# A graph network in two relational layers: which edge rows of layer one are picked by a product instead of gathered, and when they are used

## The chip, the cores and the metric

The kernel runs on one core of a Trainium2 chip. The metric is the device time of one execution in microseconds, the median over several runs.

## The reference, cut to what matters

`h` starts as `relu(layernorm(x))` (3125 nodes, 128 features). Two relational layers follow, over 100,000 edges sorted by destination `dst`, and behind them a GCN part of two convolutions, which the change doesn't touch. A relational layer is

```python
c = comp[etype]                                   # 200 relations, 8 bases
for b in range(num_bases):                        # 8
    xb = h @ V[b]
    m = m + c[:, b, None] * xb[src]
m = m * norm
agg = jax.ops.segment_sum(m, dst, num_segments=h.shape[0])
out = agg + bias + h @ loop_w
```

## The kernel before, in words

The kernel sums over edges first and multiplies by `V` afterwards. Edges come in 784 tiles of 128, in the order of their destination; 8 tiles are a chunk `c` (98 of them), 4 chunks (`j` = 0 to 3) belong to a group `g` of 128 destination nodes (25 groups). A tile needs the rows `h[src]` of its 128 edges. They land in a ring of 8 chunks. **GpSimd** fetches them with one indirect DMA for each tile (`chunk`, L831; the first chunks at L286 and L854); ahead of each chunk it waits until TensorE has finished the chunk five before it (`edges_done`).

Some tiles are not gathered but *picked*. VectorE compares the 128 source numbers of the tile with all 3200 node numbers (`make_pick`, L1016, in two halves of 13 and 12 blocks of 128 nodes, h = 0 and h = 1), which gives 25 one-hot blocks; TensorE multiplies each by the rows of `h`, split in three bf16 parts (25 products of 384 columns, all into the one bank `ps_p`); VectorE adds the three parts into the ring's slot (`keep_picked`, L1032). In layer one (`layer == 0` in the code) the last tile of every odd chunk from 5 to 95 is picked: 46 tiles, two picks a group. The pick for an odd chunk is multiplied in that chunk and the one before it, in sixths (`pick_sixth`, L1280): three pieces in each chunk. There is one buffer `pick` and one bank, so a half is only written when the previous pick's same half was multiplied, and the first product of a pick waits until the previous one was kept (`row_ready`).

In each chunk of layer one VectorE, in order, makes the one-hot edge types (L474), the match with the nodes (L972), `lo` (L978, which waits until TensorE has begun the chunk before: `m_free`), the weights `C` (L993), `M` (L983, called the keys below), then a row to keep and a half of a pick, then the sums of the coefficients (L489, L494); in the third chunk it folds the degrees of the group before (L1061 to L1063), and in the fourth it waits for their product on TensorE (L1252) and keeps it (L1067). TensorE, in order: eight products `lo` x `M` (`sum_slab`, L1219), of which the first waits for the keys, a sixth, the type products (L483), a sixth, in the fourth chunk the degrees' product, four of the chunk's eight edge tiles (L1342), a sixth, the other four tiles. In the second chunk the group's output products stand ahead (L563 to L565). ScalarE copies the results out of PSUM. The last edge tile of an odd chunk is the picked one, so its products wait for `keep_picked`, which VectorE does in the *next* chunk, behind that chunk's keys.

The groups run in a hardware loop of two groups (parity 0 and 1), with a few groups written out at either end. Layer two (`layer == 1`) has picks of its own and begins when layer one is done. SyncE issues the loads of the edge types, of the source numbers of a pick (L877), and the stores of finished slabs, in one queue.

## Time and profile before

| | us |
|---|---|
| median of 3 runs (1999.92 to 2003.72) | 2001.1 |
| the profiled execution | 1999.43 |
| its span, from the first to the last instruction | 1997.8 |
| TensorE busy in it | 1727.5 |
| VectorE busy | 1493.0 |
| GpSimd busy | 1383.6 |

Layer one runs from about 85 to 990 us, layer two and the GCN part behind it. Busy times are of a whole kernel whose parts have different limits, so they tell little about one part; the waits of a stretch, and which of them ends last, tell more.

### The profile page before, as it was taken

Reading aid. Unit: us, or ns where it says so; the run is one execution under the profiler, and the core shown is the slowest. Engines: PE = TensorE matmul, PEld = TensorE weight load, DVE = VectorE, ACT = ScalarE, POOL = GpSimd, SP = SyncE. Lnnn points to the kernel's source line nnn. Section 1 sums busy time; section 2 is a strip of 40 time slices with the busy share of each in tenths; the row PEclk is TensorE's granted clock in tenths of the full one; section 3 lists DMA queues with packets and bytes.
Section 4 is the critical chain, followed back from the end, with each engine's and each line's share of the span. In section 5 each row is a group of like instructions: output and inputs, shape, how many; then the busy total and the mean of one; then the engine's idle time right before and its main releaser. Section 6 shows DMA issues by size and latency. Waiting matters only on the chain. (4 is left out here: it accounts for less than half of the span.)

```text
span 1997.8 us, 41905 instructions
## 1 busy us (share of the span) xinstructions
PE 1727.5 (86%) x12855; PEld 1237.7 (62%) x12856; DVE 1493.0 (75%) x2360; ACT 357.1 (18%) x869; POOL 1383.6 (69%) x1505
## 2 busy tenths in 40 slices
PE   1488888888888888888659999999999999999998
PEld 1366656556556556556537777767667676676564
DVE  7898888888888888887478888877777777652533
ACT  2032222222222222222201011101011010011300
POOL 5777777777777777777477777777777777777000
PEclk8589989889889889988779999999999999989999
DMA  5334334334334334333222222233333322325473
GB/s 151 92 98 114 96 99 109 94 98 110 94 97 108 95 97 109 95 96 88 70 60 64 63 64 64 63 85 86 86 101 93 86 80 80 115 57 167 154 240 120
DMA packets 196506, 196.71 MB, mean 98 GB/s; under 512 B 109132, under 2 KB 160089, under 8 KB 196410
## 3 DMA queue, kind: packets, MB, share of 16 engines
q0 software_dynamic: 45056, 92.36, 18.1%
q1 hardware_dynamic: 143302, 99.03, 17.2%
q10 hardware_dynamic: 8052, 4.04, 0.7%
q8 instruction: 59, 0.97, 0.2%
q14 instruction: 37, 0.30, 0.0%
HBM read 169.75 MB, written 25.57 MB: 98 GB/s over the span
## 5 line engine op out<-in xcount | busy, mean ns | idle before, releaser
L831 POOL DMA_INDIRECT ring<-h_rows,rel_idx x1292 | 1239.8, 960 | 387.9 <-issue 360.2
L1016 DVE TENSOR_TENSOR rel_pick<-rel_src_row,dve_bank 128x1664 bf16<-128x1664 int32 (+1 forms) x268 | 486.2, 1815 | 104.0 <-PE rel_ps_p L1267 56.5
L1342 PE MATMUL rel_ps_z<-rel_C,ring 128*128 128x56 f32 x3100 | 404.1, 278 | 95.2 <-DVE ring L1032 76.3
L1342 PEld LDWEIGHTS rel_ps_z<-rel_C,ring 128*128 128x128 f32 x3100 | 392.1, 197 | 136.6 <-issue 125.8
L1267 PE MATMUL rel_ps_p<-rel_h_parts,rel_pick 128*128 128x384 bf16 x1650 | 283.7, 328 | 24.3 <-DVE rel_h_parts L1004 22.0
L1440 ACT ACTIVATE rel_ZT<-rel_ps_z 128x304 f32 x292 | 114.2, 426 | 1028.6 <-PE rel_ps_z L1342 1023.1
L1280 PE MATMUL rel_ps_p<-rel_h_parts,rel_pick 128*128 128x384 bf16 x1150 | 264.8, 361 | 0.0
L1267 PEld LDWEIGHTS rel_ps_p<-rel_h_parts,rel_pick 128*128 128x128 bf16 x1650 | 158.6, 100 | 138.3 <-issue 30.5
L1430 ACT ACTIVATE rel_A<-rel_ps_a 128x500 f32 x292 | 165.5, 603 | 387.3 <-PE rel_ps_a L1219 209.5
L1219 PE MATMUL rel_ps_a<-rel_M,rel_lo 128*128 128x175 bf16 x784 | 156.3, 299 | 37.1 <-DVE rel_M L983 36.9
L1267 PE MATMUL carried<-rel_h_parts,rel_pick 128*128 128x384 bf16 x1100 | 186.2, 326 | 2.4 <-DVE rel_pick L1016 2.4
L983 DVE TENSOR_TENSOR rel_M<-dve_bank,key_table 128x1400 bf16<-128x1400 f32 x98 | 157.3, 1605 | 0.0
L1267 PEld LDWEIGHTS carried<-rel_h_parts,rel_pick 128*128 128x128 bf16 x1100 | 105.9, 98 | 71.0 <-DVE rel_pick L1016 2.8
L1280 PEld LDWEIGHTS rel_ps_p<-rel_h_parts,rel_pick 128*128 128x128 bf16 x1150 | 113.5, 112 | 56.6 <-issue 22.1
L1219 PEld LDWEIGHTS rel_ps_a<-rel_M,rel_lo 128*128 128x128 bf16 x784 | 77.3, 109 | 105.9 <-issue 61.8
L854 POOL DMA_INDIRECT ring<-h_rows,idx_table x100 | 101.8, 1018 | 56.0 <-issue 33.6
L978 DVE TENSOR_TENSOR rel_lo<-dve_bank,src_lo_table 128x1024 bf16<-128x1024 f32 x98 | 119.4, 1218 | 27.2 <-PE rel_ps_a L1211 27.2
L993 DVE TENSOR_TENSOR rel_C<-dve_bank,coef 128x448 f32<-128x448 f32 x196 | 121.4, 619 | 14.4 <-PE rel_ps_z L1347 2.5
L483 PE MATMUL rel_ps<-comp_parts,rel_onehot 100*128 100x48 bf16 x1568 | 63.3, 193 | 46.3 <-DVE rel_onehot L474 28.6
L483 PEld LDWEIGHTS rel_ps<-comp_parts,rel_onehot 100*128 100x128 bf16 x1568 | 61.2, 103 | 66.1 <-DVE rel_onehot L474 28.8
L474 DVE TENSOR_SCALAR rel_onehot<-rel_types,type_id 100x1024 bf16<-100x1024 bf16 x196 | 91.8, 510 | 10.4 <-DMA rel_types<-edge_types 5.9
L1026 DVE TENSOR_TENSOR rel_pick<-rel_extra_row,dve_bank 128x1664 bf16<-128x1664 int32 (+1 forms) x44 | 79.9, 1816 | 19.6 <-PE carried L1267 19.6
(233 smaller groups left out, 1776.1 us busy)
## 6 DMA issues: line engine op xcount, KB each, us to landing
ring<-h_rows,rel_idx POOLq DMA_INDIRECT x1292
A_slabs<-rel_A SPq DMA_DIRECT2D x25, 800.0 KB
A_slot<-A_slabs SPq DMA_DIRECT2D x25, 800.0 KB, 4.5
rel_types<-edge_types SPq DMA_DIRECT2D x97, 200.0 KB
early_slot<-A_slabs SPq DMA_DIRECT2D x18, 896.0 KB, 6.3
rel_src_row<-in_src_dram SPq DMA_DIRECT2D x134, 64.0 KB, 3.0
last_slot<-A_slabs SPq DMA_DIRECT2D x4, 512.0 KB, 5.5
ring<-h_rows,idx_table POOLq DMA_INDIRECT x116
```

What stands on the lines that cost most here:

```text
L483: ins = self.nc.tensor.matmul(self.ps[:, e * 6 * NB:(e + 1) * 6 * NB], self.onehot[:, s, h, e * P:(e + 1) * P], flat(self.t.comp[:, h, :, ...
L831: g_.indirect_dma_start(ring[:, s * CHUNK + i, :], None, rows_in, bass.IndirectOffsetOnAxis(ap=idx[which][:, n:n + 1], axis=0)).then_inc(l ...
L978: v.tensor_tensor(lo[s][:, :, :], lows.unsqueeze(1).to_broadcast(shape), t.src_lo[:, bass.ds(c * CHUNK, CHUNK)].unsqueeze(2).to_broadcast( ...
L983: v.tensor_tensor(M[s][:, :, :], keys.unsqueeze(1).to_broadcast(shape), t.key[:, bass.ds(c * CHUNK, CHUNK)].unsqueeze(2).to_broadcast(shap ...
L993: v.tensor_tensor(C[s][:, :, :, :], match[s].unsqueeze(2).to_broadcast(shape), t.coef[layer][:, bass.ds(first, CHUNK), :].unsqueeze(3).to_ ...
L1016: v.tensor_tensor(pick[:, b0:b0 + n, :], src_row[s][:, :].unsqueeze(1).to_broadcast(shape), node_ids[:, b0:b0 + n].unsqueeze(2).to_broadca ...
L1219: ins = m_.matmul(into[:, :, bass.ds(half_at[h][i], TW)], lo[s][:, h * HALF + i, :], keyed(s, h * HALF + i), start=False, stop=(i == HALF ...
L1267: ins = m_.matmul(ps_p[s][:, 0:3 * P], pick[:, b, :], h_parts[:, b, :, :].rearrange("p c n -> p (c n)"), start=(b == 0), stop=(b == SRC_BL ...
L1280: ins = m_.matmul(ps_p[0][:, 0:3 * P], pick[:, b, :], h_parts[:, b, :, :].rearrange("p c n -> p (c n)"), start=(b == 0), stop=(b == SRC_BL ...
L1342: ins = m_.matmul(bank(ps_z[s], NB)[:, :, bass.ds(at[i], TW)], ring[:, first + i, :], C[s][:, i, :, :], start=False, stop=(i == n - 1))
L1430: ins = s_.activation(A[into][:, :, bass.ds(column, HN)], half_bank(ps_a[h]), ACT.Copy)
L1440: ins = s_.activation(ZT[into][:, :, bass.ds(column, CN)], bank(ps_z[s], NB), ACT.Copy)
```

## The change

Picked rows are used one chunk later: the pick that is multiplied in chunks j and j + 1 now stands for the last tile of chunk j + 2, an even one, and the even chunks gather 7 tiles, the odd ones 8. In every second group (parity 1, the odd ones) one more tile is picked, the last of its fourth chunk: this *third* pick is made from a buffer of its own (`extra_row`), is multiplied whole in the third chunk, in quarters of 7, 6, 6 and 6 blocks (`pick_quarter`), and the group's last ordinary pick is multiplied whole in the fourth chunk. That is 12 tiles more that are picked and 12 gathers fewer (4 x 7 + 3 x 8 + 7 = 59 in 8 chunks, where 60 were). The core of the diff; the waits of SyncE's loads, the semaphore counts of the ring and the calls follow from it:

```diff
@@ order of picks, and which tile of a chunk is not gathered
-        def number(g, j):
-            return 2 * g - 2 + j // 2
+        def number(g, j, parity, pair):
+            return 2 * g - 2 + j // 2 + pair + (1 if parity == 1 and j == 3 else 0)
+        def nearby(g, j, parity, by):
+            parity, pair = (parity + by) % 2, loop[1] + (parity + by) // 2
+            return number(g + by, j, parity, pair)
+        def is_third(parity, j):
+            return layer == 0 and parity == 1 and j == 2
@@ gathers
-            return CHUNK if late else CHUNK - (1 if layer == 1 else s % 2)
+            return CHUNK if late else CHUNK - (1 if layer == 1 or s == THIRD else 1 - s % 2)
@@ SyncE
+                def load_third(g, before):
+                    after(sp, pick_ready, before)
+                    rows = io["src"].rearrange("(a n) -> a n", a=1)
+                    sp.dma_start(extra_row[:, :], rows[:, bass.ds((g * CPG + 3) * (CHUNK * P) + (CHUNK - 1) * P, P)].to_broadcast([P, P]))\
+                      .then_inc(extra_in, 16)
+                            if parity == 0 and j == 0 and not is_group(g, GROUPS - 1):
+                                load_third(g + 1, 2 * nearby(g, 3, parity, -1) + 2)
@@ VectorE, a chunk of layer one
+                        third = nearby(g, 2, parity, 0)
                         if j % 2 == 0:
-                            behind = (g, 1) if j == 2 else (g - 1, 3)
                             if not (isinstance(g, int) and not first_picks(c - 1)):
-                                keep_picked(number(*behind), 0, (parity * CPG + j - 1) % SLOTS_RING * CHUNK + CHUNK - 1)
-                            if not (isinstance(g, int) and not first_picks(c + 1)):
-                                make_pick(number(g, j + 1), j // 2, g - 1, (1,))
+                                behind = nearby(g, 1, parity, 0) if j == 2 else nearby(g, 3, parity, -1)
+                                keep_picked(behind, 0, (parity * CPG + j) * CHUNK + CHUNK - 1)
+                            if is_third(parity, j):
+                                make_extra(third, loop[1], 1)
+                            elif not (isinstance(g, int) and not first_picks(c + 1)):
+                                make_pick(nearby(g, j + 1, parity, 0), j // 2, g - 1, (1,))
+                        elif parity == 1 and j == 1:
+                            make_extra(third, loop[1], 0)
+                        elif parity == 1:
+                            keep_picked(third, 0, THIRD * CHUNK + CHUNK - 1)
+                            make_pick(nearby(g, 3, parity, 0), 1, g - 1, (1,))
+                        elif j == 1:
+                            if not (isinstance(g, int) and not first_picks(c + 2)):
+                                make_pick(nearby(g, 3, parity, 0), 1, g - 1, (0,))
                         else:
-                            ahead = (g, 3) if j == 1 else (g + 1, 1)
-                            if not (isinstance(g, int) and not first_picks(c + 2)):
-                                make_pick(number(*ahead), ahead[1] // 2, ahead[0] - 1, (0,))
+                            make_pick(nearby(g, 1, parity, 1), 0, g, (0,))
...
+                    if is_third(parity, j):
+                        make_pick(nearby(g, 3, parity, 0), 1, g - 1, (0,))
                     if layer == 0 and j == 3 and not is_first:
                         keep_deg(g - 1)
+                        if parity == 1 and not is_group(g, GROUPS - 2):
+                            make_pick(nearby(g, 1, parity, 1), 0, g, (0,))
@@ TensorE
+PICK_QUARTERS = ((0, 7), (7, 13), (13, 19), (19, 25))
+            def pick_quarter(c, which):
+                b0, b1 = PICK_QUARTERS[which]
+                if which == 0:
+                    after(pe, row_ready, c)
+                if which % 2 == 0:
+                    pe.wait_ge(pick_ready, 2 * c + (1 + which // 2))
+                for b in range(b0, b1):
+                    ins = m_.matmul(ps_p[0][:, 0:3 * P], pick[:, b, :], h_parts[:, b, :, :].rearrange("p c n -> p (c n)"),
+                                    start=(b == 0), stop=(b == SRC_BLOCKS - 1))
+                if which % 2:
+                    ins.then_inc(picked, 1)
+                    quarters = picks_here and parity == 1 and j >= 2
...
-                        if layer == 0 and i == CHUNK - 1 and j % 2 == 1 and not (isinstance(c, int) and not first_picks(c)):
-                            pe.wait_ge(row_ready, number(g, j) + 1)
+                        if layer == 0 and i == CHUNK - 1 and j % 2 == 0 and not (isinstance(c, int) and not first_picks(c - 1)):
+                            pe.wait_ge(row_ready, (nearby(g, 1, parity, 0) if j == 2 else nearby(g, 3, parity, -1)) + 1)
+                        if layer == 0 and i == CHUNK - 1 and j == 3 and parity == 1:
+                            pe.wait_ge(row_ready, nearby(g, 2, parity, 0) + 1)
```

**VectorE, end of the fourth chunk of an odd group.** The rows of before: the second coefficient product, the degrees that it waits for, the loop's branch and the next group's types.

```order
L494 TENSOR_TENSOR coef<-rel_summed,norm_table 128x64
L1067 REGISTER_ALU [waits rel0_deg_done]
L1067 TENSOR_SCALAR deg<-rel_ps_h 128x1
L727 REGISTER_ALU
L727 COMPARE_AND_BRANCH
L474 TENSOR_SCALAR rel_onehot<-rel_types,type_id 100x1024 [waits rel0_types_in2,rel0_product_done]
```

The same place now:

```order
L496 TENSOR_TENSOR coef<-rel_summed,norm_table 128x64
L1089 REGISTER_ALU [waits rel0_deg_done]
L1089 TENSOR_SCALAR deg<-rel_ps_h 128x1
L92 ISA [waits rel0_src_row_in0]
L1038 TENSOR_TENSOR rel_pick<-rel_src_row,dve_bank 128x1664 [waits rel0_picked]
L729 REGISTER_ALU
L729 COMPARE_AND_BRANCH
L476 TENSOR_SCALAR rel_onehot<-rel_types,type_id 100x1024 [waits rel0_types_in2,rel0_product_done]
```

The first half of the next group's pick, which stood ahead of the coefficients, is made behind the degrees.

**VectorE, from the fold of the degrees (third chunk of an odd group) to the fourth chunk's types.** Before:

```order
L1061 TENSOR_TENSOR rel_A<-rel_A 128x12x128 [waits rel0_deg_done,rel0_a_out]
L1061 TENSOR_TENSOR rel_A<-rel_A 128x6x128 [waits rel0_deg_chain]
L1061 TENSOR_TENSOR rel_A<-rel_A 128x3x128 [waits rel0_deg_chain]
L1062 TENSOR_TENSOR rel_A<-rel_A 128x2x128 [waits rel0_deg_chain]
L1063 TENSOR_TENSOR rel_deg_sum<-rel_A 128x128 [waits rel0_deg_chain]
L474 TENSOR_SCALAR rel_onehot<-rel_types,type_id 100x1024 [waits rel0_types_in1,rel0_product_done]
```

Now:

```order
L1083 TENSOR_TENSOR rel_A<-rel_A 128x12x128 [waits rel0_deg_done,rel0_a_out]
L1083 TENSOR_TENSOR rel_A<-rel_A 128x6x128 [waits rel0_deg_chain]
L1083 TENSOR_TENSOR rel_A<-rel_A 128x3x128 [waits rel0_deg_chain]
L1084 TENSOR_TENSOR rel_A<-rel_A 128x2x128 [waits rel0_deg_chain]
L1085 TENSOR_TENSOR rel_deg_sum<-rel_A 128x128 [waits rel0_deg_chain]
L92 ISA [waits rel0_src_row_in1]
L1038 TENSOR_TENSOR rel_pick<-rel_src_row,dve_bank 128x1664 [waits rel0_picked]
L476 TENSOR_SCALAR rel_onehot<-rel_types,type_id 100x1024 [waits rel0_types_in1,rel0_product_done]
```

A half of a pick, of 1664 columns, is new between the fold and the types.

**TensorE, fourth chunk of an odd group, from the type products to the first edge tile.** Before:

```order
L483 MATMUL rel_ps<-comp_parts,rel_onehot 128x48 [waits rel0_onehot_ready]
L483 MATMUL rel_ps<-comp_parts,rel_onehot 128x48 x15
L1280 MATMUL rel_ps_p<-rel_h_parts,rel_pick 128x384 x4
L1161 ISA
L1161 TENSOR_LOAD pe_row
L1252 MATMUL rel_ps_h<-ones,rel_deg_sum 128x1 [waits rel0_h_new,rel0_deg_kept,rel0_deg_summed]
L1235 ISA
L1342 REGISTER_ALU [waits rel0_c_ready,ring_odd]
L1342 MATMUL rel_ps_z<-rel_C,ring 128x8x7
```

Now:

```order
L485 MATMUL rel_ps<-comp_parts,rel_onehot 128x48 [waits rel0_onehot_ready]
L485 MATMUL rel_ps<-comp_parts,rel_onehot 128x48 x15
L1314 MATMUL rel_ps_p<-rel_h_parts,rel_pick 128x384 x6
L1196 ISA
L1196 TENSOR_LOAD pe_row
L1287 MATMUL rel_ps_h<-ones,rel_deg_sum 128x1 [waits rel0_h_new,rel0_deg_kept,rel0_deg_summed]
L1312 REGISTER_ALU
L1314 MATMUL rel_ps_p<-rel_h_parts,rel_pick 128x384 [waits rel0_pick_ready]
L1314 MATMUL rel_ps_p<-rel_h_parts,rel_pick 128x384 x5
L1270 REGISTER_ALU
L1401 REGISTER_ALU [waits rel0_c_ready,ring_odd]
L1401 MATMUL rel_ps_z<-rel_C,ring 128x8x7
```

The piece ahead of the degrees' product has 6 products for 4 (the one ahead of the type products 7 for 4), and a piece of 6 is new behind it.

**TensorE, last two edge tiles of the fourth chunk of an even group.** Before:

```order
L1342 ISA
L1342 MATMUL rel_ps_z<-rel_C,ring 128x8x7
L1342 ISA [waits rel0_row_ready]
L1342 MATMUL rel_ps_z<-rel_C,ring 128x8x7
L1180 MATMUL rel_ps_z<-zero 128x304 [waits rel0_zt_kept]
L1347 ISA
L1347 MATMUL rel_ps_z<-rel_C,ring 128x8
```

Now:

```order
L1401 ISA
L1401 MATMUL rel_ps_z<-rel_C,ring 128x8x7
L1401 ISA
L1401 MATMUL rel_ps_z<-rel_C,ring 128x8x7
L1215 MATMUL rel_ps_z<-zero 128x304 [waits rel0_zt_kept]
L1406 ISA
L1406 MATMUL rel_ps_z<-rel_C,ring 128x8
```

The wait for the kept row is gone here (and in every second chunk).

## Rows read from the trace of the kernel before

**Rows 1.** The page: busy time, share of the span and count, by engine

```profile
PE 1727.5 (86%) x12855; PEld 1237.7 (62%) x12856; DVE 1493.0 (75%) x2360; ACT 357.1 (18%) x869; POOL 1383.6 (69%) x1505
```

**Rows 2.** Waits from 140 to 880 us: us in total, times, longest

```profile
PE rel_ps_z L1342 <- DVE ring L1032: 68.5, 40, 3.6
PE rel_ps_a L1219 <- DVE rel_M L983: 29.9, 19, 1.8
...
DVE deg L1067 <- PE rel_ps_h L1252: 47.8, 20, 2.7
DVE ring L1032 <- PE rel_ps_p L1280: 22.5, 20, 1.2
DVE rel_lo L978 <- PE rel_ps_a L1211: 21.9, 20, 1.2
DVE rel_pick L1016 <- PE rel_ps_p L1280: 18.8, 20, 1.1
...
POOL ring L831 <- issue: 163.0, 548, 0.3
```

**Rows 3.** GpSimd: gathers from 442.7 us on (busy, count), and its timeline (start, us)

```profile
442.70:978.90 536.20, 406.60 (x420) 0.90 0.38 98
...
413.48 0.95 POOL L831 DMA_INDIRECT ring<-h_rows,rel_idx  x1 [0.30 <-issue]
...
415.98 1.15 POOL L831 DMA_INDIRECT ring<-h_rows,rel_idx  x1 [0.30 <-issue]
...
442.80 0.22 POOL L803 COPY rel_idx<-idx_table 128x32 int32 x1
```

**Rows 4.** The end of layer one: TensorE's timeline

```profile
967.19 0.42 PE L1342 MATMUL rel_ps_z<-rel_C,ring 128*128 128x56 f32 x2 [1.90 <-DVE ring L1032]
...
973.03 3.63 PE L1342 MATMUL rel_ps_z<-rel_C,ring 128*128 128x56 f32 x16 [3.10 <-DMA ring<-h_rows,rel_idx]
```

**Rows 5.** VectorE's timeline in group 9 (odd): start, us, [idle before]

```profile
404.26 0.54 DVE L1032 TENSOR_REDUCE ring<-rel_ps_p 128x128 f32<-128x384 f32 x1
404.73 1.74 DVE L1016 TENSOR_TENSOR rel_pick<-rel_src_row,dve_bank 128x1536 bf16<-128x1536 int32 x1
...
412.52 1.89 DVE L1016 TENSOR_TENSOR rel_pick<-rel_src_row,dve_bank 128x1664 bf16<-128x1664 int32 x1 [0.79 <-PE rel_ps_p L1280]
...
417.48 1.23 DVE L978 TENSOR_TENSOR rel_lo<-dve_bank,src_lo_table 128x1024 bf16<-128x1024 f32 x1 [1.04 <-PE rel_ps_a L1211]
...
421.88 0.56 DVE L1032 TENSOR_REDUCE ring<-rel_ps_p 128x128 f32<-128x384 f32 x1 [1.12 <-PE rel_ps_p L1280]
...
437.14 0.16 DVE L1067 TENSOR_SCALAR deg<-rel_ps_h 128x1 f32 x1 [2.53 <-PE rel_ps_h L1252]
...
441.86 0.56 DVE L1032 TENSOR_REDUCE ring<-rel_ps_p 128x128 f32<-128x384 f32 x1
```

**Rows 6.** TensorE's timeline in the same group

```profile
406.09 0.95 PE L1219 MATMUL rel_ps_a<-rel_M,rel_lo 128*128 128x175 bf16 x4
...
425.20 0.98 PE L1280 MATMUL rel_ps_p<-rel_h_parts,rel_pick 128*128 128x384 bf16 x5
...
426.43 0.81 PE L1280 MATMUL rel_ps_p<-rel_h_parts,rel_pick 128*128 128x384 bf16 x4
...
432.00 0.86 PE L1219 MATMUL rel_ps_a<-rel_M,rel_lo 128*128 128x175 bf16 x4 [1.58 <-DVE rel_M L983]
...
442.62 0.42 PE L1342 MATMUL rel_ps_z<-rel_C,ring 128*128 128x56 f32 x2 [3.41 <-DVE ring L1032]
```

**Rows 7.** Busy by engine in four stretches; last three: clock, DMA, GB/s

```profile
406.00:409.00 3.00, 3.00 (x16) 1.62 (x15) 2.86 (x8) 1.71 (x5) 2.39 (x3) 0.50 0.37 67
410.00:433.00 23.00, 20.12 (x175) 15.04 (x173) 19.61 (x29) 4.48 (x11) 17.65 (x20) 1.00 0.46 117
433.50:436.30 2.80, 2.80 (x26) 1.63 (x25) 0.97 (x4) 0.00 (x0) 2.19 (x3) 0.50 0.24 57
437.00:443.00 6.00, 2.59 (x22) 2.27 (x22) 5.40 (x9) 2.19 (x4) 4.78 (x6) 1.00 0.35 89
```

More of the change, by code:

```diff
@@ L850, in _ @@
                     stage(0, SLOTS_RING)
-                for i in range(c * CHUNK, c * CHUNK + (CHUNK if layer == 0 and c < 4 else gathers(c))):
+                for i in range(c * CHUNK, c * CHUNK + (CHUNK if layer == 0 and c < FIRST_PICK else gathers(c))):
                     if i % HALF == 0:
@@ L1023, in make_extra @@
                     dve.wait_ge(extra_in, (turn + 1) * 16)
[L1024 removed]
+                after(dve, picked, 2 * k + (h - 1))
                 shape = [P, n, P]
```

40 lines of the change are left out of this document (25 added, 15 removed).

## Prediction

> **What bounds the kernel now.** The page names TensorE as the busiest engine (1727.5 us) [rows 1], but the change is made in layer one, so the waits of 140 to 880 us come first. Nobody waits for a gather there. TensorE waits for VectorE, 68.5 us for kept rows and 29.9 for keys, and VectorE waits for TensorE, 47.8 + 22.5 + 21.9 + 18.8 us; GpSimd waits for nobody and has only its 0.3 us of issue ahead of each gather [rows 2]. So there are two trains that run side by side, each at its own pace, and the reader has to find which is late at the end.
>
> GpSimd: from 442.7 to 978.9 us it issues 420 gathers, 536.2 us, 1.277 us for one [rows 3]; a group of 30 takes 38.3 us. A plain gather costs 0.95 + 0.30 = 1.25 us [rows 3].
>
> TensorE with VectorE: TensorE gets the row of chunk 39 at 442.62 [rows 6] and that of chunk 95 at 967.19 [rows 4]: 14 groups in 524.6 us, 37.5 us a group, so this train is the faster one. At 442.80, when chunk 39's last products are just under way, GpSimd copies the indices of chunk 42 [rows 3]: it leads by two chunks. That lead shrinks by 0.8 us a group and is used up only at the end: the only long wait for a landing is 3.10 us ahead of chunk 96, whose tiles are multiplied at 973.03 [rows 4]. So the present time is the pace of the TensorE/VectorE train, with 3 us of GpSimd on top. Fewer gathers by themselves are worth 3 us; what the edit does to the pace of the other train decides the rest.
>
> The timeline of one group shows that pace. VectorE goes from 404.26 to 441.86, 37.6 us, with four waits, 0.79 + 1.04 + 1.12 + 2.53 = 5.5 us [rows 5], so it works 32.1 us and has the tighter schedule. TensorE waits 1.58 us for the keys of the fourth chunk and 3.41 us for the row of its last tile [rows 6]. Its granted clock is 1.00 of 2.4 GHz, but 0.50 (1.2 GHz) right behind each of these two waits (406 to 409 and 433.5 to 436.3) [rows 7].
>
> **The change, part by part.** Pairs of groups are counted, an even and an odd one; there are 11.5 between chunk 4 and chunk 96.
>
> *Gathers.* 12 fewer, 12 x 1.25 = 15.0 us. With the present gaps chunk 96 would have landed at 973.0 - 15.0 = 958.0. TensorE would be there without any wait at 973.0 - 3.1 = 969.9. To be there at 958.0, its train must gain 12 / 11.5 = 1.04 us a pair.
>
> *VectorE's added work.* A kept row takes 0.47 us (404.26 to 404.73); the halves take 1.74 and 1.89 [rows 5], of which about 0.08 lies under the next instruction, so 1.66 and 1.81. Together 3.94 us a pair, in the odd group. VectorE has no free time at which this could be hidden except its four waits.
>
> *TensorE's added work.* 25 products. Five take 0.98 and four 0.81 [rows 6], 0.17 for one: 4.25 us a pair, in the odd group's third and fourth chunk. In the third chunk 12 more than now, 2.0 us, lie beside VectorE's longer chunk, under the wait for the next keys (1.58 now, and these keys come 1.81 later). In the fourth, 3 + 2 = 5 of them stand ahead of the degrees' product, for which VectorE waits already (2.53): VectorE is let go 0.85 us later at full clock, 1.7 at half. This wait hides the row and the half (0.47 + 1.66 in place of 1.81) ahead of it, but not the half of 1.81 that now stands behind it, nor the one of 1.81 behind the fold. So an odd group costs VectorE 1.81 + 1.81 + 0.85 = 4.5 us at full clock, up to 5.3 at half.
>
> *What is given back.* Today, after the keys of a group's first chunk, TensorE still waits for the row, then does two edge products, the clearing and the transposition, and begins the chunk's `lo` x `M` at 406.09 [rows 6]. The keys were done when the kept row began, at 404.26 [rows 5], and a release takes some 0.2 us (442.42 to 442.62) [rows 5, 6]. With the row's wait moved behind, TensorE has that tail done before and begins at about 404.5, 1.57 us sooner. All of the first and second chunk on TensorE comes sooner by this, so the waits of 0.79 and 1.04 shrink by 1.57 together: 3.14 us a pair. If the 1.2 GHz stretch behind the old 3.41 us wait goes too, TensorE has up to 1.7 us more (3 us of work at half speed), of which VectorE can use what is left of its waits in these chunks, 0.26 + 1.12 = 1.4 us: up to 2.8 a pair.
>
> Does that stretch go? The 3.41 us wait doesn't vanish whole: TensorE now waits for the first chunk's keys. From the degrees' answer VectorE needs 441.86 - 437.14 = 4.7 us to them [rows 5]; TensorE reaches them some 3.4 sooner than it did the release, so it waits about 1.3 us after an even group, and about 1.8 us after an odd one (1.81 later keys, 8 products more). The 1.58 us wait today is followed by 1.2 GHz [rows 6, 7], so these will in part be too. I take half of the 2.8.
>
> *Sum.* Best: 4.5 - 3.14 - 2.8 = -1.4 us a pair. Worst: 5.3 - 3.14 = +2.2. Middle: 4.9 - 3.14 - 1.4 = +0.4. I take 0, as 0.4 is within the error of the terms. Over 11.5 pairs: -16, 0, +25 us. Then chunk 96 has landed at 958 and TensorE comes at 969.9: only the 3.1 us wait goes.
>
> *At nothing.* SyncE's 12 added loads of 64 KB and their waits: the row buffer is free when its pick was made, and in an even group SyncE now waits for this until late in the group before, with the next types' load behind it; those are wanted more than a chunk (9 us) later, which is the cover. Without it, types late by x us would stop VectorE by x. Odd chunks with 8 gathers and even ones with 7: the lead of two chunks hides it. Layer two and all behind it is the same program and begins sooner or later with layer one's end.
>
> A rule weighed. The gather at 415.98 takes 1.15 us, that at 413.48, beside a half of a pick (412.52), 0.95 [rows 3, 5]: so I let the added halves cost GpSimd nothing. The Trainium skill ("GPSIMD Engine Reference", section 1, Specifications) says that GpSimd shares its SBUF interfaces with VectorE, with contention beside instructions in a two-port mode or with two SBUF inputs, which speaks against any VectorE work added to save gathers. The pick's second input lies in the PSUM bank, and the row agrees that it doesn't count. Were it to count with the 0.2 us of the slow gather, 24 halves would take back 24 x 0.2 = 4.8 of the 15.0 us, and the sum would stay, since GpSimd isn't what ends last.
>
> The profiled execution took 1999.43 us, so this gives 1999.4 - 3 = 1996.4; the runs' median is 1.7 above that execution: 1998.
>
> **The rivals.**
> *Gathers become the bound, all or most of them are gained.* If the train gains 1.04 us a pair or more, chunk 96 is multiplied at 958 and the whole gain is 15.0 us: 2001.1 - 15 = 1986. For: the best case above is beyond that point; the 3.41 us wait is the longest of TensorE's. Against: it needs nearly all 1.2 GHz stretches of the first chunks gone. Half of it (gain of 0.5 a pair) gives 1992.
> *Slower: VectorE's 3.94 us a pair cost more than TensorE's earlier start gives.* One mechanism: TensorE's four waits for keys in a pair (1.3, 1.58, about 1.4, 1.8 us) each bring a 1.2 GHz stretch, so none of the 2.8 us comes back and the degrees of the odd group are late by 1.7. It is slower than now as soon as a pair costs +0.3 (11.5 x 0.3 = the 3.1 us). At +1.3, between middle and worst, 15 - 3 = +12: 2013; at worst 2023. For: VectorE has the fullest schedule, and the row of 1.58 us with 0.50 behind it. Against: the longest wait is cut.
> *The change doesn't do what it says:* should the kept row still come late (its copy is behind the same keys), TensorE would wait 0.5 us there and nothing else changes: the second chunk's row wait today is only 0.2 us. Inside the first range.
>
> **How the numbers follow.** As now, less 3 us (a pair within -0.4 to +0.5 us): 0.45, 1994 to 2003 for the median. Gathers bound or half way to it: 0.31, 1985 to 1993. Slower: 0.21, 2004 to 2023. Something else: 0.03. The range leaves out the last of the best and the upper part of the slower case: 1985 to 2011. A measurement of this kernel tells about 0.2%, 4 us, from no change. Faster by more: 0.31 and a quarter of the first case, 0.42. Slower by more: 0.21 less its lower edge, 0.20. Within: 0.38.
>
> **What the profile after would show.** Right: the wait of TensorE for kept rows, 68.5 us, falls to under 10, and that for keys grows from 29.9 to about 100 to 130 (four waits in 10 pairs); VectorE's waits for `lo` and for picked halves nearly go, that for the degrees stays at 40 to 60; a pair of groups takes about 75 us; no wait for a landing at the end, and GpSimd is done about 15 us sooner, before TensorE. Wrong towards faster: pairs of under 74 us, waits for landings in many late chunks. Wrong towards slower: pairs of 76 us or more, a granted clock below today's in layer one, GpSimd held by `edges_done`. A late load of types or sources, or a wait of VectorE for a pick's first half in the third chunk, would be a wait that I have not priced.

## The result, and the profile after

The changed kernel takes 2008.97 us (median of 9 runs, 2006.54 to 2015.62), the kernel before 2001.02 (9 runs, 1996.44 to 2003.72). The ratio is 1.0051, with a 95% interval of 1.0041 to 1.0061: slower by 0.5%. I had forecast 3 us less. The time lies in my range, but on the side to which I gave 0.20.

The page of the changed kernel, first line of its part 1 (busy time, share, count), answers to [rows 1]:

```profile
PE 1748.1 (87%) x13155; PEld 1253.9 (62%) x13156; DVE 1535.8 (77%) x2396; ACT 356.6 (18%) x869; POOL 1369.7 (68%) x1493
```

GpSimd has 12 instructions less, TensorE 300 products and 20.6 us more, VectorE 36 instructions and 42.8 us more. Waits from 140 to 880 us, to be laid beside [rows 2]:

```profile
POOL ring L842 <- issue: 163.2, 530, 3.2
...
PE rel_ps_a L1254 <- DVE rel_M L1005: 89.1, 40, 2.9
DVE deg L1089 <- PE rel_ps_h L1287: 54.0, 20, 3.8
...
DVE ring L1054 <- PE rel_ps_p L1328: 21.6, 19, 1.3
...
DVE rel_lo L1000 <- PE rel_ps_a L1246: 14.8, 19, 1.1
...
DVE rel_onehot L476 <- issue: 0.2, 1, 0.2
```

TensorE's 68.5 us of waits for rows are gone, but those for keys went from 29.9 to 89.1: of 98.4 us only 9 went away. VectorE's 18.8 us for picked halves are gone. It still waits for `lo` and for the pick that it keeps, and for the degrees longer than before. In this stretch it gave up some 21 us of waits.

These rows give VectorE's account for a pair of groups, if the 740 us are taken as 9.9 pairs before and 9.7 now. Its busy time grew by 42.8 us over 12 third picks, 3.6 each. Its wait for the degrees went from 4.8 to 5.6. Against this, the waits for picked halves went from 1.9 to nothing, those for `lo` from 2.2 to 1.5, and a pause ahead of the edge types from 0.4 to nothing (this row before):

```profile
DVE rel_onehot L474 <- issue: 3.9, 9, 0.5
```

Together +3.6 + 0.7 - 1.9 - 0.7 - 0.4 = +1.3 us a pair.

VectorE in group 9, the same group as in [rows 5]:

```profile
428.17 1.22 DVE L1000 TENSOR_TENSOR rel_lo<-dve_bank,src_lo_table 128x1024 bf16<-128x1024 f32 x1 [0.96 <-PE rel_ps_a L1246]
...
432.56 0.56 DVE L1054 TENSOR_REDUCE ring<-rel_ps_p 128x128 f32<-128x384 f32 x1 [1.12 <-PE rel_ps_p L1328]
433.04 1.75 DVE L1048 TENSOR_TENSOR rel_pick<-rel_extra_row,dve_bank 128x1536 bf16<-128x1536 int32 x1
...
444.11 0.55 DVE L1054 TENSOR_REDUCE ring<-rel_ps_p 128x128 f32<-128x384 f32 x1
...
450.27 0.16 DVE L1089 TENSOR_SCALAR deg<-rel_ps_h 128x1 f32 x1 [2.98 <-PE rel_ps_h L1287]
```

And TensorE around it, to be laid beside [rows 6]: it now waits for keys four times in a pair of groups.

```profile
444.37 0.86 PE L1254 MATMUL rel_ps_a<-rel_M,rel_lo 128*128 128x175 bf16 x4 [2.81 <-DVE rel_M L1005]
449.86 0.28 PE L1287 MATMUL rel_ps_h<-ones,rel_deg_sum 128*128 128x1 f32 x2
...
456.76 0.87 PE L1254 MATMUL rel_ps_a<-rel_M,rel_lo 128*128 128x175 bf16 x4 [2.33 <-DVE rel_M L1005]
...
483.21 0.98 PE L1254 MATMUL rel_ps_a<-rel_M,rel_lo 128*128 128x175 bf16 x4 [2.26 <-DVE rel_M L1005]
...
492.53 0.95 PE L1254 MATMUL rel_ps_a<-rel_M,rel_lo 128*128 128x175 bf16 x4 [1.57 <-DVE rel_M L1005]
```

The clock behind the first of these waits, to be laid beside [rows 7] (stretch, its length, busy by engine, granted clock, DMA, GB/s):

```profile
427.00:441.00 14.00, 13.88 (x134) 10.59 (x133) 11.64 (x20) 3.02 (x6) 10.82 (x11) 1.00 0.25 71
441.60:444.40 2.80, 0.03 (x1) 0.04 (x1) 2.80 (x4) 0.25 (x2) 2.11 (x3) 1.00 0.18 47
444.40:447.00 2.60, 2.60 (x13) 1.37 (x14) 2.46 (x4) 0.00 (x0) 1.99 (x3) 0.65 0.20 50
```

The clock stays at 1.00 through the wait and falls behind it, at the first products after the keys. It is so behind each of the four:

```profile
445.50:448.50 3.00, 3.00 (x16) 1.48 (x14) 1.64 (x4) 0.00 (x0) 2.39 (x3) 0.50 0.27 64
459.00:462.00 3.00, 3.00 (x25) 1.88 (x24) 2.85 (x8) 1.09 (x2) 2.08 (x4) 0.50 0.34 73
483.00:486.00 3.00, 2.79 (x13) 1.66 (x14) 2.65 (x5) 0.00 (x0) 2.30 (x3) 0.50 0.21 53
493.20:496.20 3.00, 3.00 (x18) 1.62 (x18) 2.86 (x7) 2.18 (x4) 2.39 (x3) 0.50 0.23 56
```

Before, a pair had four such waits too, one for a row and one for keys in each group [rows 6, 7]. In a fourth chunk the 1.2 GHz stretch stands ahead of the degrees' product, for which VectorE waits.

**Where the time went.** The best mark in the traces is the transposed product that TensorE does when it has used a chunk's tiles. Its start, in us:

| after chunk | before | changed | difference |
|---|---|---|---|
| 4 | 118.9 | 121.2 | +2.3 |
| 8 | 154.1 | 161.0 | +6.9 |
| 16 | 226.3 | 235.7 | +9.4 |
| 56 | 601.4 | 616.6 | +15.2 |
| 88 | 901.1 | 920.2 | +19.1 |
| 96 | 976.7 | 983.4 | +6.7 |

Three parts: +9.4 us up to chunk 16 (6.9 of them by chunk 8), +9.7 in the nine pairs from 16 to 88, and -12.4 in the last eight chunks. At the end of the program it is +8.6 (spans of 1997.8 and 2006.4), so layer two adds 1.9.

The steady part, five pairs from chunk 16 to 56, before and changed:

```profile
226.30:601.40 375.10, 312.69 (x2614) 226.19 (x2612) 308.42 (x481) 96.61 (x210) 287.75 (x309) 0.91 0.39 101
```
```profile
235.70:616.60 380.90, 324.56 (x2737) 237.49 (x2737) 325.75 (x495) 96.34 (x210) 290.39 (x313) 0.90 0.39 100
```

375.1 / 5 = 75.0 us and 380.9 / 5 = 76.2 us a pair. From the granted clock the time at 1.2 GHz follows as (1 - clock) / 0.5 of the stretch: 0.18 x 75.0 = 13.5 us a pair before, 0.20 x 76.2 = 15.2 now. The two digits of the clock leave some 0.75 us of each open, and over all nine pairs (chunk 16 to 88) both windows have 0.91. No 1.2 GHz went away.

The last part is an error of reading. The waits from 880 to 985 us in the kernel before have this row:

```profile
PE rel_ps_z L1342 <- DMA ring<-h_rows,rel_idx: 8.8, 4, 3.3
```

There were four waits for landings in the last eight chunks, 2.04, 0.43, 3.28 and 3.10 us, and I had priced only the last. The changed kernel has none, and it does these eight chunks in 63.2 us, where the kernel before takes 75.6. GpSimd issues 60 gathers in 76.8 us, so before it was GpSimd that set this part. Its last gather of layer one:

```profile
977.86 0.94 POOL L831 DMA_INDIRECT ring<-h_rows,rel_idx  x1 [0.30 <-issue]
```
```profile
966.51 0.94 POOL L842 DMA_INDIRECT ring<-h_rows,rel_idx  x1 [0.31 <-issue]
```

Counted through the trace, the last gather of chunk 96 is issued 6.3 us ahead of the transposed product before, which is what a chunk takes that waits for its landing, and that of chunk 88 already only 7.1 us ahead. In the changed kernel these are 24.7 and 37.2 us.

### The profile page after: what moved, and what is told of

Read it like the earlier page. It is cut to its first block and busy times, and to the rows that moved or that the text cites. A ratio compares the mean times of both kernels' runs of the same rounds, so it can differ in the third digit from the quotient of the medians.

```text
span 2006.4 us, 42673 instructions
## 1 busy us (share of the span) xinstructions
PE 1748.1 (87%) x13155; PEld 1253.9 (62%) x13156; DVE 1535.8 (77%) x2396; ACT 356.6 (18%) x869; POOL 1369.7 (68%) x1493
## 5 line engine op out<-in xcount | busy, mean ns | idle before, releaser
L842 POOL DMA_INDIRECT ring<-h_rows,rel_idx x1280 | 1224.0, 956 | 390.5 <-issue 358.6
L1401 PE MATMUL rel_ps_z<-rel_C,ring 128*128 128x56 f32 x3100 | 389.7, 275 | 11.5 <-DMA ring<-h_rows,rel_idx 4.6
L1302 PE MATMUL rel_ps_p<-rel_h_parts,rel_pick 128*128 128x384 bf16 x1650 | 283.2, 328 | 24.6 <-DVE rel_h_parts L1026 22.3
L1302 PEld LDWEIGHTS rel_ps_p<-rel_h_parts,rel_pick 128*128 128x128 bf16 x1650 | 158.6, 100 | 138.2 <-issue 30.2
L1254 PE MATMUL rel_ps_a<-rel_M,rel_lo 128*128 128x175 bf16 x784 | 141.3, 291 | 101.9 <-DVE rel_M L1005 101.8
L1328 PE MATMUL rel_ps_p<-rel_h_parts,rel_pick 128*128 128x384 bf16 x850 | 199.8, 366 | 0.2
L1254 PEld LDWEIGHTS rel_ps_a<-rel_M,rel_lo 128*128 128x128 bf16 x784 | 72.7, 108 | 161.1 <-issue 125.8
L1048 DVE TENSOR_TENSOR rel_pick<-rel_extra_row,dve_bank 128x1664 bf16<-128x1664 int32 x68 | 123.3, 1814 | 20.9 <-PE carried L1302 19.7
L1015 DVE TENSOR_TENSOR rel_C<-dve_bank,coef 128x448 f32<-128x448 f32 x196 | 121.2, 619 | 14.9 <-PE rel_ps_z L1406 2.6
L1314 PE MATMUL rel_ps_p<-rel_h_parts,rel_pick 128*128 128x384 bf16 x600 | 122.5, 350 | 0.0
L1328 PEld LDWEIGHTS rel_ps_p<-rel_h_parts,rel_pick 128*128 128x128 bf16 x850 | 84.9, 113 | 43.8 <-issue 20.8
```

The costliest lines, as they stand in the source:

```text
L842: g_.indirect_dma_start(ring[:, s * CHUNK + i, :], None, rows_in, bass.IndirectOffsetOnAxis(ap=idx[which][:, n:n + 1], axis=0)).then_inc(l ...
L1015: v.tensor_tensor(C[s][:, :, :, :], match[s].unsqueeze(2).to_broadcast(shape), t.coef[layer][:, bass.ds(first, CHUNK), :].unsqueeze(3).to_ ...
L1048: v.tensor_tensor(pick[:, b0:b0 + n, :], extra_row[:, :].unsqueeze(1).to_broadcast(shape), node_ids[:, b0:b0 + n].unsqueeze(2).to_broadcas ...
L1254: ins = m_.matmul(into[:, :, bass.ds(half_at[h][i], TW)], lo[s][:, h * HALF + i, :], keyed(s, h * HALF + i), start=False, stop=(i == HALF ...
L1302: ins = m_.matmul(ps_p[s][:, 0:3 * P], pick[:, b, :], h_parts[:, b, :, :].rearrange("p c n -> p (c n)"), start=(b == 0), stop=(b == SRC_BL ...
L1314: ins = m_.matmul(ps_p[0][:, 0:3 * P], pick[:, b, :], h_parts[:, b, :, :].rearrange("p c n -> p (c n)"), start=(b == 0), stop=(b == SRC_BL ...
```

## The experiments

Each kernel ran against the kernel before on one chip. "Pair" is from the transposed products, chunk 16 to 56 unless another stretch is given, and the clock is that of the same stretch. cheap_halves, cheap_products and fill_waits were run more than once; the table has their last runs.

| kernel | median us | ratio to before | pair us | clock |
|---|---|---|---|---|
| before | 2001.02 | 1 | 75.0 | 0.91 |
| changed | 2008.97 | 1.0051 (1.0041 to 1.0061) | 76.2 | 0.90 |
| later_only | 2004.35 | 1.0022 (1.0012 to 1.0032) | 71.8 (16 to 40) | 0.93 |
| wait_back | 2045.99 | 1.0226 (1.0211 to 1.024) | 79.9 | 0.90 |
| deg_early | 1990.33 | 0.9955 (0.9939 to 0.9972) | 72.4 | 0.93 |
| before_deg_early | 2003.16 | 1.0017 (1.0006 to 1.0027) | 67.7 (8 to 24) | 0.96 |
| cheap_halves | 2000.74 | 0.9983 (0.9973 to 0.9994) | 75.4 | 0.90 |
| cheap_products | 1997.95 | 0.998 (0.9967 to 0.9994) | 75.1 | 0.89 |
| cheap_both | 1995.08 | 0.9979 (0.9967 to 0.9991) | 73.3 | 0.86 |
| fill_waits | 1996.06 | 0.9981 (0.9969 to 0.9993) | 73.2 | 1.00 |
| deg_fill | 1989.16 | 0.9942 (0.9925 to 0.9959) | 71.2 (16 to 40) | 1.00 |

### One half of the change alone: later_only

```diff
-            return 2 * g - 2 + j // 2 + pair + (1 if parity == 1 and j == 3 else 0)
+            return 2 * g - 2 + j // 2
...
 def is_third(parity, j):
-            return layer == 0 and parity == 1 and j == 2
+            return False
...
-                    quarters = picks_here and parity == 1 and j >= 2
+                    quarters = False
```

(The third picks' loads, halves, kept rows and waits go with them, and each odd chunk gathers its eight tiles.)

> One half of the change alone: a picked row is used one chunk later, and there are 46 picks as before, each in sixths over two chunks, so that the gathers are as many as before. My theory now: VectorE's 3.94 us of third pick a pair are what made the changed kernel slower, and the earlier start of TensorE is a true gain; then the train of TensorE and VectorE takes 72 to 74 us a pair, GpSimd's gathers become what ends layer one, waits for landings stand ahead of many late chunks, and the time is that of the kernel before: ratio 0.997 to 1.001 (1995 to 2003 us). Rival, the move itself costs (four waits for keys a pair, each with 1.2 GHz behind it, in place of two waits for rows): pairs of 75 us or more, no waits for landings, 2001 to 2010 us.

Measured: 2004.35 us, 1 us past the upper edge of what the theory gave and inside the rival's range, but with the theory's signs, faster pairs and waits for landings. Up to chunk 40 a pair takes 71.8 us, and from there 75.7 to 78.5. Waits from 140 to 880 us:

```profile
PE rel_ps_z L1389 <- DMA ring<-h_rows,rel_idx: 58.4, 39, 3.4
...
PE rel_ps_a L1244 <- DVE rel_M L1002: 41.1, 27, 2.6
```

Follows: using the rows later is a gain of 75.0 - 71.8 = 3.2 us a pair for the train, and the third pick costs 76.2 - 71.8 = 4.4. The clock is part of both: it is 0.93 here, 0.91 before and 0.90 in the changed kernel. GpSimd needs 76 to 77 us for the gathers of a pair, so the faster the train, the sooner GpSimd's lead is used up: 39 waits for landings of 58.4 us, where the kernel before has 1.0 us of them in the same stretch. The rival, that the move itself costs, falls.

### The old wait put back: wait_back

```diff
+                        if layer == 0 and i == CHUNK - 1 and j % 2 == 1 and not (isinstance(c, int) and not first_picks(c)):
+                            pe.wait_ge(row_ready, nearby(g, j, parity, 0) + 1)
```

> The changed kernel, with TensorE's old wait for the kept row put back ahead of the last edge product of every second and fourth chunk. If the earlier start gives what I worked out (3.14 us a pair, and up to 2.8 of clock), a pair takes 79 to 81 us in place of 76 and the time is 2040 to 2065 us. Rival, the earlier start is worth nothing because TensorE only exchanges the wait for the row against one for keys: 2005 to 2015 us, and the wait for keys shrinks by what the wait for rows takes.

Measured: 2045.99 us, 79.9 us a pair, 3.7 more than the changed kernel. Waits from 140 to 880 us:

```profile
PE rel_ps_z L1403 <- DVE ring L1054: 65.4, 37, 3.8
...
PE rel_ps_a L1254 <- DVE rel_M L1005: 34.0, 19, 2.3
```

Both are as the theory gave them. Follows: TensorE's waits have nearly the sum of the kernel before (99.4 us; 98.4 there, 89.1 in the changed kernel), and 37 us of time hang on where they stand. The earlier start is worth 3.2 (with later_only) to 3.7 us a pair. The clock is the same 0.90 from chunk 16 to 56, so there this is the order alone. Over chunk 16 to 88 the difference is 3.2 us a pair, with a clock of 0.93 from chunk 56 on.

### The degrees' product a chunk's work earlier: deg_early and before_deg_early

```diff
+                    if layer == 0 and j == 3 and not is_first:
+                        degrees(g - 1)
                     if layer == 0:
                         sum_slab(c, j % 2, at)
...
-                    if layer == 0 and j == 3 and not is_first:
-                        degrees(g - 1)
```

> The changed kernel, with TensorE's degrees' product of a fourth chunk put ahead of that chunk's lo x M products (its operand is ready a chunk earlier), so that VectorE no longer waits for it: 54 us of waits between 140 and 880 us. If VectorE's full schedule sets the pace, a pair takes 71.5 to 74 us in place of 76, the 12 fewer gathers now count, and the time is 1984 to 1994 us, faster than both kernels, with waits of TensorE for landings in the late chunks. Rival, TensorE's products set the pace (its 25 more products a pair, and 1.2 GHz): a pair stays at 75.5 to 76.5 and the time at 2005 to 2011 us, VectorE's wait only moves to its lo.

> The kernel before, with the same move of the degrees' product. Its train gains as much, but it has all 736 gathers of the old plan: the theory that GpSimd is only 3 us behind the train gives 1997 to 2002 us (ratio 0.998 to 1.001), with waits for landings in the late chunks, and so says that 12 fewer gathers are worth their 15 us only beside this. Rival, gathers are no bound near here: 1985 to 1992 us.

Measured: 1990.33 us for deg_early, faster than both kernels. VectorE's wait for the degrees isn't in the list any more, and TensorE waits for landings in the late chunks. Waits from 140 to 880 us of deg_early:

```profile
PE rel_ps_a L1254 <- DVE rel_M L1005: 59.1, 28, 2.8
...
DVE rel_pick L1038 <- PE rel_ps_p L1314: 29.0, 11, 3.5
...
PE rel_ps_z L1401 <- DMA ring<-h_rows,rel_idx: 12.1, 12, 2.7
```

The same for before_deg_early:

```profile
PE rel_ps_z L1342 <- DMA ring<-h_rows,rel_idx: 44.7, 31, 2.8
```

It takes 2003.16 us, 1 us past the upper edge of what the theory gave, though its train needs only 67.7 us a pair from chunk 8 to 24, until GpSimd is caught; the kernel before takes 73.5 there.

Follows: the same move, with all of TensorE's and VectorE's work kept, gives 3.8 us a pair to the changed kernel. On the kernel before, a train that is 5.8 us a pair faster gives nothing, because GpSimd ends the layer. The two together are worth 10 us, and each alone loses: the change 8 us, the move 2 to 3. A part of the 3.8 is clock, 0.93 in place of 0.90; the last experiment splits it. (The 736 gathers in that text are my count for layer one; only the difference of 12 matters.)

### Whose work the third pick's 4.4 us are: cheap_halves, cheap_products, cheap_both

```diff
 make_extra, VectorE:
+                if layer == 0:
+                    n = 1
...
 pick_quarter, TensorE:
-                for b in range(b0, b1):
+                for b in (b0, b1 - 1):
```

> The changed kernel, but VectorE's two halves of a third pick compare only one block of 128 nodes each in place of 13 and 12 (what TensorE multiplies for that pick is then the old content, so those rows aren't the right ones). TensorE's products, the waits, the loads and the gathers stay. This takes 3.2 to 3.4 us of VectorE's work out of a pair and leaves the kept row (0.47). If VectorE's added work sets what the third pick costs (a pair went from 71.5 us with the rows used later alone to 76.0 with the third pick), a pair falls to 72 to 73.3 us, GpSimd's gathers bound the late chunks, and the time is 1984 to 1993 us. Rival, TensorE's 25 added products cost it: pairs stay at 75 to 76 us and the time at 2003 to 2010.

> The changed kernel, but TensorE does only two products for each quarter of the picks done in the third and fourth chunk of every second group: 16 in place of 50 a pair, 34 x 0.17 = 5.8 us less than the changed kernel and 1.5 us less than the kernel before (those picked rows aren't the right ones). VectorE's work, the waits and the gathers stay. If VectorE's added work sets the cost, only the part of it that TensorE hands on falls away, the product of the degrees 0.85 us (now 1.4 with 8 fewer ahead of it) sooner: pairs of 74.5 to 75.5 us, 1996 to 2005 us. Rival, TensorE's added products are the cost: pairs of 72 to 73 us, and 1984 to 1993 us.

> cheap_halves and cheap_products together: VectorE compares one block for each half of a third pick, TensorE does 16 in place of 50 products in the quarters (those picked rows aren't the right ones); waits, loads, kept rows and gathers stay. If the two engines' added work lie side by side in one loop of waits, each as long as the other, a pair falls from 76.1 us (75.1 with either cut alone) to 71.5 to 73.5 us, the gathers bind the late chunks, and the time is 1984 to 1992 us. Rival, the third pick costs by its order and its waits (whole picks in quarters, a kept row in the fourth chunk): a pair stays at 74.3 to 75.1 us, and the time at 1996 to 2001 us.

(34 of 50 products go in the second edit, 9 more than the third pick brought.)

The first two were run four times. In the first three the kernel before took 2580 to 2608 us (last section), and these kernels 2539.24, 2539.32 and 2560.75 (cheap_halves) and 2537.43, 2533.2 and 2559.05 us (cheap_products), which tells nothing of the question: their pairs took 93.7 to 95.5 us there. What was written ahead of the second, third and fourth:

> The same kernel as cheap_halves again, since that group of three ran on a chip on which the kernel before took 2580 us in place of 2001 and every kernel's pair about 94 us. VectorE's two halves of a third pick compare one block of 128 nodes each in place of 13 and 12 (those picked rows aren't the right ones). If VectorE's added work sets what the third pick costs, a pair takes 72 to 73.3 us until the gathers bound it, and the time is 1984 to 1993 us. Rival, TensorE's 25 added products cost it: pairs stay at 75 to 76 us and the time at 2003 to 2010.

> The same kernel as cheap_products again: two products for each quarter of the picks in the third and fourth chunk of every second group, 16 in place of 50 a pair, 5.8 us less on TensorE (those picked rows aren't the right ones). If VectorE's added work sets the cost, only the product of the degrees comes 0.85 to 1.4 us sooner: pairs of 74.5 to 75.5 us, 1996 to 2005 us. Rival, TensorE's added products are the cost: pairs of 72 to 73 us, and 1984 to 1993 us.

> cheap_halves again. If VectorE's added work sets what the third pick costs, a pair takes 72 to 73.3 us until the gathers bound it, and the time is 1984 to 1993 us. Rival, TensorE's 25 added products cost it: pairs of 75 to 76 us and 2003 to 2010 us. On a chip on which the kernel before takes 2580 us: 2540 us again, which says nothing.

> cheap_products again. If VectorE's added work sets the cost: pairs of 74.5 to 75.5 us, 1996 to 2005 us. Rival, TensorE's added products are the cost: pairs of 72 to 73 us, and 1984 to 1993 us.

> cheap_halves on another chip. If VectorE's added work sets what the third pick costs, a pair takes 72 to 73.3 us until the gathers bound it, and the time is 1984 to 1993 us. Rival, TensorE's 25 added products cost it: pairs of 75 to 76 us and 2003 to 2010 us.

> cheap_products on another chip. If VectorE's added work sets the cost: pairs of 74.5 to 75.5 us, 1996 to 2005 us. Rival, TensorE's added products are the cost: pairs of 72 to 73 us, and 1984 to 1993 us.

The numbers here are from the fourth: 2000.74 us and 75.4 us a pair for cheap_halves, 1997.95 and 75.1 for cheap_products. Neither gives 72 to 73. cheap_products lies inside what the theory gave for it; cheap_halves misses the theory's pair, and its time lies between the two ranges. Waits from 140 to 880 us, cheap_halves:

```profile
PE rel_ps_a L1256 <- DVE rel_M L1005: 81.8, 40, 2.6
...
DVE rel_lo L1000 <- PE rel_ps_a L1248: 35.1, 20, 2.8
```

and cheap_products:

```profile
PE rel_ps_a L1254 <- DVE rel_M L1005: 112.9, 39, 4.7
```

Follows: my theory that VectorE's work alone is the cost falls, and the rival with TensorE's too. With 3.1 us a pair less on VectorE (1535.8 - 1498.4 us of busy time over 12 third picks), VectorE waits 20.3 us more for `lo`, that is, for TensorE. With 5.8 less on TensorE (34 x 0.17, at full clock), TensorE waits 23.8 us more for keys. Each saving goes into a wait for the other engine, and 0.8 to 1.1 us a pair is left. Both cuts together (1995.08 us) give 76.2 - 73.3 = 2.9, more than 0.8 + 1.1 = 1.9. That fits two engines side by side in one loop, each waiting for the other, but it is 1.5 us short of the 4.4, and the time missed both ranges. The window of its five pairs says why in part:

```profile
230.30:596.80 366.50, 307.21 (x2568) 226.59 (x2567) 310.66 (x496) 96.08 (x210) 279.53 (x298) 0.86 0.41 102
```

A clock of 0.86 is 0.28 x 73.3 = 20.5 us a pair at 1.2 GHz, 5.3 more than in the changed kernel: by my estimate 2.6 us of TensorE's savings were taken back by its slower clock (half of 5.3, as the work takes twice as long there). What is left of the gap, the kept row of 0.47 us and the order of the quarters, wasn't taken apart.

cheap_products shows something else too. At chunk 88 its train is 3.8 us later than that of the kernel before (904.9 us), at chunk 96 it is 8.2 us earlier (968.5), and TensorE waits for no landing in between. So with 12 fewer gathers the end came sooner although the train was no faster until then.

### The waits filled with products of zeros: fill_waits

```diff
                         ins.then_inc(m_free, 1)
+                        for _ in range(fill):
+                            m_.matmul(ps_a[0][:, 0:SRC_BLOCKS * HN], t.zero16[:, 0:P], t.zero16[:, 0:SRC_BLOCKS * HN], start=False, stop=False)
                         pe.wait_ge(m_ready, c + 1)
...
+                        sum_slab(c, j % 2, at, 0 if is_first or is_last else (8, 0, 0, 11)[j])
```

> The changed kernel, with products of zeros added onto the first bank of A while TensorE waits for the keys: 8 in each first chunk of a group, 11 in each fourth (0.21 us each, 1.7 and 2.3 us, behind the transposed product that frees VectorE's lo). They keep TensorE busy through most of the waits of 1.6 to 2.8 us. If the 1.2 GHz behind these waits takes the missing 1.4 to 2.8 us a pair, as my prediction priced it, the granted clock in the pairs rises from 0.91 to 0.97 or more, a pair falls to 73.5 to 75 us and the time to 1990 to 2000. Rival, the clock is paid only where VectorE has waits that it can't use, so that it hardly counts: pairs of 75.7 to 76.5 us, 2004 to 2012 us, with the clock up.

> The same kernel as fill_waits again: products of zeros while TensorE waits for the keys of a group's first and fourth chunk. If the 1.2 GHz behind these waits takes the missing 1.4 to 2.8 us a pair, the granted clock in the pairs rises from 0.91 to 0.97 or more, a pair falls to 73.5 to 75 us and the time to 1990 to 2000. Rival, the clock hardly counts, because VectorE is what is waited for: pairs of 75.7 to 76.5 us, 2004 to 2012 us, with the clock up.

> fill_waits again. If the 1.2 GHz behind the waits for keys takes the missing 1.4 to 2.8 us a pair, the granted clock in the pairs rises from 0.91 to 0.97 or more, a pair falls to 73.5 to 75 us and the time to 1990 to 2000. Rival, the clock hardly counts: pairs of 75.7 to 76.5 us, 2004 to 2012 us, with the clock up.

> fill_waits on another chip: products of zeros while TensorE waits for the keys of a group's first and fourth chunk. The changed kernel has 14.5 us a pair at 1.2 GHz, the kernel before 13.6. If the 1.2 GHz behind the waits for keys is what is missing of my sum, these 14.5 us fall to under 8, a pair falls from 76.1 to 73.5 to 75 us, and the time to 1986 to 2000. Rival, the clock hardly counts, since VectorE is waited for anyway: pairs of 75.7 to 76.5 us, 2004 to 2012 us, with less time at 1.2 GHz.

The first three, where the kernel before took 2580 to 2608 us, took 2544.21, 2545.95 and 2572.57 us. Measured in the last: 1996.06 us, within what was given, and 73.2 us a pair, a little under it. The window of the five pairs and the waits from 140 to 880 us:

```profile
229.00:595.20 366.20, 345.86 (x2927) 240.40 (x2926) 326.18 (x496) 96.27 (x210) 280.42 (x301) 1.00 0.41 102
```
```profile
DVE deg L1089 <- PE rel_ps_h L1289: 38.2, 21, 1.9
...
PE rel_ps_a L1256 <- DVE rel_M L1005: 9.9, 20, 0.6
PE rel_ps_z L1403 <- DMA ring<-h_rows,rel_idx: 6.5, 10, 1.2
```

Follows: the clock is at 2.4 GHz throughout, and with all the work of the changed kernel, plus 38 products of zeros, a pair is 3.0 us shorter. VectorE's wait for the degrees falls from 54.0 to 38.2 us. So the 1.2 GHz stretches cost the changed kernel 3.0 us a pair, and with them gone it takes 4 us less than the kernel before as it stands, ratio 0.9981 (0.9969 to 0.9993). The same filling wasn't tried on the kernel before, which has as much 1.2 GHz.

### Both: deg_fill

The two edits together.

> deg_early and fill_waits together: the degrees' product ahead of the fourth chunk's, and products of zeros in the waits for keys. The train gains from both: pairs of 69 to 71 us until GpSimd is caught, earlier than in deg_early (about chunk 30 in place of chunk 56), and then 76 to 78 us a pair. If the gathers are then all that binds, the time is that of deg_early, 1986 to 1992 us, with more waits for landings. Rival, the gathers are still ahead and the train still counts: 1975 to 1985 us.

Measured: 1989.16 us, the same as deg_early within the intervals, with 71.2 us a pair up to chunk 40 and 13 waits for landings (16.5 us) from 140 to 880 us in place of 12 (12.1 us). Follows: a train that is faster by another 1.1 us a pair (72.3 in deg_early up to chunk 40) gives nothing. What is left is most likely GpSimd, with 12 gathers fewer, and the time is close to the 1986 of my rival. It is the best version found, with deg_early, which does it without products that compute nothing.

It also splits deg_early's 3.8 us. With the clock at 1.00 in both, up to chunk 40, the move takes a pair from 73.2 (fill_waits) to 71.2: 2.0 us are the move's own, and about 1.8 came with the better clock.

## Why the prediction was wrong

- **"The present time is the pace of the TensorE/VectorE train, with 3 us of GpSimd on top."** Right from chunk 16 to 88, where nobody waits for a landing in either kernel, wrong behind it. In the last eight chunks the train can run at 63.2 us, and GpSimd, whose lead was used up by chunk 88, held it at 75.6. So fewer gathers were worth up to 12.4 us there (8.8 us of it waits for landings), not 3, and the train didn't have to gain 1.04 us a pair first: cheap_products has the gain with a train no faster. later_only and before_deg_early speed the train and gain nothing, which says the same: GpSimd ended layer one before. No kernel was run that takes the gathers away and adds nothing.
- **TensorE's earlier start, 3.14 us a pair.** Right in size: 3.2 (later_only, with a clock of 0.93 for 0.91) and 3.7 (wait_back, at the same clock).
- **The third pick, 4.5 to 5.3 us.** Right in size: 4.4. The reason was half of it. I let VectorE's work set it, with TensorE's through the degrees; cutting either gives about 1 us, which fits one loop of both. VectorE's work grew by 3.6 us for each third pick, not 3.94, and its wait for the degrees by 0.7.
- **The failing step: half of the 2.8 us from 1.2 GHz stretches that vanish.** None vanished: 13.5 us a pair before, 15.2 after, the same 0.91 over chunks 16 to 88. A pair had four long waits of TensorE before and has four now, each with 0.50 behind it. I wrote that the waits for keys would be about 1.3 and 1.8 us in the first chunks, 1.58 and 1.4 in the fourth. In the pair shown above they are 1.57 and 2.33, 2.26 and 2.81. They add up to 9.0 us a pair in place of 6.1, nearly as much as the waits for rows and keys together before (98.4 us in 740, 10.0 a pair [rows 2]), and the chip went to 1.2 GHz behind them as it had behind those. Why they are longer is only in part known: in group 9 VectorE's waits of 0.79 and 1.04 us [rows 5] became one of 0.96, so it used 0.87 of the 1.57 us by which TensorE came sooner, and the 0.7 left over fit the wait of 2.26 that I had left at 1.58. fill_waits shows the price: with the clock kept at 1.00 a pair takes 3.0 us less. With 0 in place of 1.4 my middle would have been 4.9 - 3.14 = +1.8, and with the measured terms it is 4.4 - 3.2 = +1.2, which is what the windows show from chunk 16 to 56 (+1.1 up to 88).
- **"I take 0, as 0.4 is within the error of the terms."** This second step moved the forecast to the side of no change, though slower began at +0.3 a pair. The sum's own middle lay on the slower side of that line.
- **11.5 equal pairs.** Wrong at both ends. Until chunk 16 the change costs 9.4 us. With later_only chunk 8 is 0.9 us late (155.0) and chunk 16 is 0.8 us early (225.5), so nearly all of this start comes with the first third picks. The granted clock from 108 to 118 us is 0.50 and 0.55 in the changed kernel, 0.91 and 1.00 before; why it stayed down there was not tried. In the last eight chunks, where VectorE makes its last edge types (at 915 us before, 935 now), the change gave 12.4 us back, not 3.
- **The range held by luck.** By chunk 88 the train was 19.1 us late, where I had 0, and behind it 12.4 us came back, where I had 3. These two errors have opposite signs, and the 8 us between the medians are about what they left, with 1.9 us from layer two that nothing here explains.
- **Signs.** Right: no waits for rows, none for picked halves, degrees at 54, no landing wait at the end. Wrong: GpSimd done 11.4 us sooner (977.86 and 966.51), not 15, keys 89.1 (I said 100 to 130), `lo` still 14.8 of 21.9, and the kept rows' wait for the pick as before (21.6 of 22.5), which I hadn't named. A pair of 76.2 us and a clock of 0.90 were among my signs of the slower rival, and this is that rival: priced at +1.3 a pair, found at +1.2.
- **The rule weighed** ("GPSIMD Engine Reference", section 1, Specifications, of the Trainium skill) made no difference here: 60 gathers of layer one take 76.8 us on GpSimd before and 77.0 now (from its 200th to its 640th instruction of this kind), so the added halves hardly slowed it. The trace agrees with taking the rule's contention at nothing for compares with an operand in PSUM: from 140 to 880 us the gathers that lie mostly beside a half of a pick take 0.94 us before and 0.95 now. Those that lie mostly beside the fold of the degrees (`rel_A`, two inputs in SBUF) take 1.20 and 1.16 us, which agrees with the rule too.

## What to carry to other kernels

Where two engines hand work to each other, count the loop, not one engine: the same move of a single small product gave 3.8 us a pair (2.0 of it at the same clock), and cutting 3.1 us of VectorE's or 5.8 us of TensorE's work gave about 1. For a third engine that runs ahead (here GpSimd with its gathers), follow its lead to the last chunk of the layer, where the other two can be faster than on average: that end decides what fewer gathers are worth, and whether a faster loop is worth anything. Here a faster loop alone gained nothing, fewer gathers with a slower loop lost, and both together gained 10 us. When one wait replaces another on TensorE, price the clock behind the new one as that behind the old: here waits of 1.57 to 2.81 us were each followed by 1.2 GHz, as those of 1.58 and 3.41 us had been.

## What was not expected of the hardware

- Less work on TensorE came with a worse clock: 0.90 with the full picks, 0.89 with 34 products a pair fewer, 0.86 with VectorE's halves cut as well (where TensorE also waits 21.0 us for landings from 140 to 880 us). With 38 products of zeros more it was 1.00, and the kernel faster by 13 us.
- On three chips (with the first three runs of cheap_halves, cheap_products and fill_waits) the kernel before took medians of 2580 to 2608 us, and the others 2533 to 2573. One of the chips later gave 2001 for it again. VectorE was busy as long as ever (1535.9 us in fill_waits's second run, 1536.3 in its last), but TensorE's busy time was 2040.2 us in place of 1806.9, with a granted clock of 0.86 in place of 0.96, and it stood idle in the middle of rows of products that wait for nobody, as here in the second run:

```profile
588.49 0.18 PE L485 MATMUL rel_ps<-comp_parts,rel_onehot 100*128 100x48 bf16 x1 [0.46 <-issue]
589.90 0.24 PE L485 MATMUL rel_ps<-comp_parts,rel_onehot 100*128 100x48 bf16 x3 [1.23 <-issue]
590.61 0.32 PE L1330 MATMUL rel_ps_p<-rel_h_parts,rel_pick 128*128 128x384 bf16 x1 [0.48 <-issue]
```

Instructions that arrive late would look like this, but nothing here shows it. In that condition all three variants came out 1.3 to 1.9% faster than the kernel before, so a ranking from it would have said the opposite of the one above.
